# Moving the last three output products of a head pair's upper tiles behind the next step's scores

## The reference

```python
h = layernorm(x) * (1 + ca) + sa
q = rope(h @ Wq.T)                    # 32 heads of 128
c_kv = h @ Wdk.T                      # shared low rank part of keys and values
k = [rope part from h @ Wkr.T, rest from c_kv @ Wupk.T]   # 8 key heads
v = c_kv @ Wupv.T                     # 8 value heads, 4 query heads share one
a = softmax(causal(q @ k.T / sqrt(128))) @ v
x = x + ga * (a @ Wo.T)
h = layernorm(x) * (1 + cb) + sb
s = softmax(h @ router_w.T + router_b)        # 64 experts, the 8 largest kept as w
x = x + gb * (h * sum(w) + w @ expert_bias)
```

## Time and profile before

| | us |
|---|---|
| median of 3 runs (lowest, highest) | 1481.37 (1480.51, 1482.84) |
| profiled execution, time | 1481.78 |
| profiled execution, span from first to last instruction | 1480.1 |
| TensorE busy | 1451.2 (98% of the span) |
| its weight loads busy | 1211.3 (82%) |
| VectorE busy | 1160.1 (78%) |
| GpSimd busy | 1023.6 (69%) |
| ScalarE busy | 1005.0 (68%) |

### The profile page before, as it was taken

How to read it: one execution, slowest core, us unless ns; L and a number is a source line. 1 busy time by engine, 2 the same in 40 slices (tenths; PEclk the granted TensorE clock), 3 DMA queues, 4 the chain that set the end, 5 groups by cost and what they waited for, 6 DMA issues and landing times.

```text
span 1480.1 us, 24295 instructions
## 1 busy us (share of the span) xinstructions
PE 1451.2 (98%) x7012; PEld 1211.3 (82%) x7012; DVE 1160.1 (78%) x3549; ACT 1005.0 (68%) x2381; POOL 1023.6 (69%) x802
## 2 busy tenths in 40 slices
PE   7997999999999999999999999999999999999997
PEld 4686888888888888888888888888888888888876
DVE  5867777777777777777777777777779988988866
ACT  2467776776767776777677766767677676776674
POOL 1656776776667776677678666767588888886662
PEclk9999999999999999999999999999999999999999
DMA  9647775776766676578667756669788899889881
GB/s 328 205 126 255 223 229 144 213 224 182 202 216 214 181 223 188 172 219 237 182 184 222 220 168 199 213 180 254 224 248 252 270 293 260 278 263 266 268 228 51
DMA packets 214820, 322.02 MB, mean 218 GB/s; under 512 B 42248, under 2 KB 132104, under 8 KB 214688
## 3 DMA queue, kind: packets, MB, share of 16 engines
q1 hardware_dynamic: 214352, 320.34, 72.3%
q10 hardware_dynamic: 336, 0.12, 0.0%
HBM read 179.43 MB, written 140.95 MB: 216 GB/s over the span
## 4 chain that ended last, share of the span: by engine, by line
PE 90%; DVE 5%; issue 2%; ACT 2%; POOL 1%; DMA 0%; SPq 0%; DVEq 0%; ACTq 0%; POOLq 0%
PE bank_s L589 22%; PE bank_o L718 22%; PE bank_pv L696 14%; PE bank_s L649 13%; PE bank_s L617 6%; PE bank_s L602 5%; PE bank_s L560 2%; PE bank_o L523 1%; PE bank_s L645 1%; PE bank_s L771 1%; DVE blocks L1417 1%; ACT probs L1028 1%; PE bank_pv L589 1%; DMA wup_in<-in_wup 0%; PE bank_s L646 0%
## 5 line engine op out<-in xcount | busy, mean ns | idle before, releaser
L1759 POOL TENSOR_TENSOR PT_lo<-PT_raw,PT_hi 128x640 fp32r<-128x640 f32 x246 | 382.1, 1574 | 27.0 <-ACT PT_hi L1049 27.0
L1035 ACT ACTIVATE probs<-probs,row_inv 128x512 f32<-128x512 f32 (+3 forms) x512 | 258.0, 553 | 195.2 <-DVE row_inv L1400 195.1
L1747 POOL TENSOR_TENSOR rot_c<-rot_c,rot_s 128x512 f32<-128x512 f32 x128 | 166.0, 1297 | 274.3 <-DVE rot_s L1357 274.3
L1028 ACT ACTIVATE probs<-probs,row_min 128x512 f32<-128x512 f32 (+3 forms) x512 | 281.8, 552 | 52.2 <-DVE row_min L1393 52.1
L1417 DVE STREAM_TRANSPOSE blocks<-probs 128x384 f32<-128x384 f32 x508 | 213.9, 447 | 18.7 <-ACT probs L1035 12.4
L649 PE MATMUL bank_s<-kT_both,qT_hi 128*128 128x512 f32 (+2 forms) x768 | 214.9, 341 | 1.2 <-POOL qT_lo L1752 0.6
L1393 DVE CUSTOM_DVE_ANT_0 probs<-bank_s,mask 128x512 f32<-128x512 f32 (+2 forms) x384 | 203.5, 552 | 0.4
L589 PE MATMUL bank_s<-hT_lo,wq_hi 128*128 128x512 f32 x488 | 196.5, 403 | 2.5 <-DVE row_min L1393 1.2
L1752 POOL TENSOR_TENSOR qT_lo<-rot_c,qT_hi 128x512 fp32r<-128x512 f32 x128 | 166.6, 1301 | 42.2 <-ACT qT_hi L1010 41.3
L718 PE MATMUL bank_o<-wo_lo,OT_hi 128*128 128x512 f32 x496 | 194.4, 392 | 0.0
L718 PE MATMUL bank_o<-wo_hi,OT_hi 128*128 128x512 f32 x496 | 193.3, 390 | 0.0
(11 more groups left out here) (296 smaller groups left out, 3216.6 us busy)
## 6 DMA issues: line engine op xcount, KB each, us to landing
blocks<-blocks SPq DMA_DIRECT2D x127, 640.0 KB, 3.4
PT_raw<-blocks SPq DMA_DIRECT2D x500, 160.0 KB, 3.9
stage<-in_wq SPq DMA_DIRECT2D x32, 256.0 KB, 5.1
vblocks<-kv_raw SPq DMA_DIRECT2D x32, 256.0 KB, 5.4
kv_raw<-vblocks SPq DMA_DIRECT2D x128, 64.0 KB, 2.1
stage<-in_wo SPq DMA_DIRECT2D x32, 256.0 KB, 5.0
split_wq<-wq_hi SPq DMA_DIRECT2D x32, 256.0 KB, 5.4
split_wq<-wq_lo SPq DMA_DIRECT2D x32, 256.0 KB, 5.7
```

The source lines that it names most:

```text
L1028: ins = act.activation(row(t, qt), row(t, qt), ACT.Exp, bias=row_min[m][:, qt:qt + 1], scale=-1.0, accum_out=row_sum[m][:, qt:qt + 1])
L1035: ins = act.activation(row(t, qt), row(t, qt), ACT.Copy, scale=row_inv[t % 2][:, qt:qt + 1])
L1747: pool.tensor_tensor(rot_c[:], rot_c[:], rot_s[:], ALU.add).then_inc(pool_a, 1)
L1759: pool.tensor_tensor(lo[:, at], raw_of(t)[:, at], hi[:, at].bitcast(F32), ALU.subtract).then_inc(pool_t, 1)
```

## The change

In the 61 even steps t = 4 to 124, the last three of the twelve output products of the upper tiles (tile 3, second head of the pair) are no longer issued at the end of the odd step; the even step issues them between its scores and its query projection. The semaphores that tell that the upper tiles' products are done (`pe_op`, `pe_upper`) are counted up there. ScalarE's copy of the lower tiles moves from the start of the even step to between the exponentials of tiles 3, 2 and those of tiles 1, 0, and VectorE's half moves behind the maxima of tiles 1 and 0. No instruction is added or removed.

```diff
+            def upper_in_two(p):
+                return p < PAIRS - 2
+
             def out_pair(p, tiles, some=None):
...
                     for h in heads:
-                        o_at = (2 * (j - tiles[0]) + h % 2) * P
-                        for n, (o, w) in enumerate(passes(OT_of(p, tiles), wo)):
-                            mm = pe.matmul(bank[f"o{j}"][:], o[:, o_at:o_at + P], w[:, h, :], ...)
-                    if heads[1] == GROUP - 1:
-                        mm.then_inc(pe_op, 1)
-                    elif j == UPPER[-1]:
-                        mm.then_inc(pe_upper, 1)
+                        if j == UPPER[-1] and h == heads[1] and upper_in_two(p):
+                            return
+                        out_head(p, tiles, j, h)
+
+            def out_head(p, tiles, j, h):
+                u = 2 * p // GROUP
+                o_at = (2 * (j - tiles[0]) + h % 2) * P
+                for n, (o, w) in enumerate(passes(OT_of(p, tiles), wo)):
+                    mm = pe.matmul(bank[f"o{j}"][:], o[:, o_at:o_at + P], w[:, h, :], ...)
+                if h == GROUP - 1:
+                    mm.then_inc(pe_op, 1)
+                elif h == 1 and j == UPPER[-1]:
+                    mm.then_inc(pe_upper, 1)
...
# TensorE, step
                 scores(t + 1, QUERY_ORDER, before, n)
                 if h % 2 == 1 and t > 1:
                     values_pair(t // 2 - 1, LOWER)
+                if h % 2 == 0 and t > 2 and upper_in_two(t // 2 - 2):
+                    p = t // 2 - 2
+                    out_head(p, UPPER, UPPER[-1], 2 * p % GROUP + 1)
                 if 2 < t < ALL - 3:
                     q_proj(t + 3)
...
# ScalarE, step
-                if h % 2 == 0 and 2 < t < ALL - 2:
-                    pair_split_hi(t // 2 - 2, LOWER)
...
                 exponentials(t + 1, 0)
                 if h == 1 and t > 1:
                     v_split_hi(u)
+                if h % 2 == 0 and 2 < t < ALL - 2:
+                    pair_split_hi(t // 2 - 2, LOWER)
                 exponentials(t + 1, 1)
...
# VectorE, step
+                mask_and_max(t + 1, 1)
                 if h % 2 == 0 and 2 < t < ALL - 2:
                     pair_split_lo(t // 2 - 2, LOWER)
-                mask_and_max(t + 1, 1)
```

More of the change, by code:

```diff
@@ L715, in out_pair @@
                     for h in heads:
-                        o_at = (2 * (j - tiles[0]) + h % 2) * P
-                        for n, (o, w) in enumerate(passes(OT_of(p, tiles), wo)):
-                            mm = pe.matmul(bank[f"o{j}"][:], o[:, o_at:o_at + P], w[:, h, :],
-                                           start=(u < LAST_UNIT and h == 0 and n == 0),
-                                           stop=(u < LAST_UNIT - 1 and h == GROUP - 1 and n == 2))
-                    if heads[1] == GROUP - 1:
-                        mm.then_inc(pe_op, 1)
-                    elif j == UPPER[-1]:
-                        mm.then_inc(pe_upper, 1)
+                        if j == UPPER[-1] and h == heads[1] and upper_in_two(p):
[5 more added lines that the diff above has]
+                for n, (o, w) in enumerate(passes(OT_of(p, tiles), wo)):
+                    mm = pe.matmul(bank[f"o{j}"][:], o[:, o_at:o_at + P], w[:, h, :],
+                                   start=(u < LAST_UNIT and h == 0 and n == 0),
+                                   stop=(u < LAST_UNIT - 1 and h == GROUP - 1 and n == 2))
+                if h == GROUP - 1:
+                    mm.then_inc(pe_op, 1)
+                elif h == 1 and j == UPPER[-1]:
+                    mm.then_inc(pe_upper, 1)
             def values_last(t, tiles):
```

## The result

| | before | after |
|---|---|---|
| median of the runs, us | 1481.66 (4 runs, 1480.51 to 1482.84) | 1495.52 (4 runs, 1494.23 to 1496.88) |
| profiled execution, us | 1481.78 | 1495.23 |
| its span, us | 1480.1 | 1493.6 |

The ratio of the times is 1.0094, with a 95% interval of 1.0076 to 1.0111: the change makes the kernel 13.9 us slower. The forecast was 1496.5.

A forecast was written before the change was run, and what follows sets the result against it. It took TensorE's own work (busy 98%) as the bound. Terms -5.5 + 6.8 + 9.8 + 4.1 = +15.2 us on 1481.78 gave 1497.0, stated as 1496.5 for the median; range by its bounds 1490 to 1502, 8 in 10 1484.5 to 1502.

The forecast's parts named there:

- gap after the scores: TensorE, even steps: moved products fill its wait before the query projection, net 0.09 us in 61 steps, 5.5 us gain.
- key wait, quiet h = 2: Scores' tile 2: earlier weight load waits for VectorE's key rotation, 0.31 us lost in 22 steps, 6.8 us.
- late copies, t = 4 to 92: Lower output products wait for copies behind exponentials where a DMA holds ScalarE's split: 6.5 + 0.3 + 0.6 + 1.4 us.
- late copy at t = 124: Step t = 124: the split's DMA landing is late again, so the lower copy is too, 1.0 us lost.
- router steps, over the gap gain: Steps t = 94 to 122, VectorE nearly full: key and value waits lose 4.1 us, bounds 1 and 9.
- VectorE's own queue: 0: Inverses and query rotation queued behind VectorE's moved half of the copy: its idle time absorbs the hold, 0 us.
- 0.2 us in all: Late copies in the router steps: router products give them over a microsecond more, so only 0.2 us is lost.
- Rival D: Knock-on: VectorE's held queue delays rotations and landings, twenty more late steps at 0.5 us, 1506, or 1511 with slow clock; chance 0.08.
- B: Rival: key wait happens, but copies stay hidden as DMAs land earlier, +5 us, 1486; chance 0.15.
- C: Rival: lower copies come late but the scores have no key wait, +5 us, 1487; chance 0.05.
- A: Rival: only the gaps after the scores go, so faster by 5.5 to 9 us, 1474; chance 0.09.
- clock part of D: TensorE drops to the slow clock after ten waits of over half a microsecond, 1.5 us each, giving 1511.

The follow-up runs named there:

- E4: The changed kernel with ScalarE's copy of the lower tiles placed between the split and the exponentials of tiles 3 and 2; 1484.82 us.
- E6: The kernel of E4 with one product moved in the steps h = 2 instead of three, still three in h = 0; 1477.57 us.
- E1: The kernel before with only the two copies of the lower tiles moved as in the change, the three products left in the odd step; 1493.16 us.
- E9: The kernel before, no product moved: ScalarE's copy between split and exponentials, VectorE's half behind the maxima of tiles 1 and 0; 1481.64 us.
- E8: The kernel before with only VectorE's half of the lower tiles' copies moved, behind the maxima of tiles 1 and 0; 1480.76 us.
- E12: The changed kernel with one product moved in the steps h = 2 instead of three, copies left as in the change; 1491.06 us.
- E7: The kernel of E4 with two products moved in the steps h = 2 instead of three; 1479.96 us.

## Why the prediction was right, and where it was right only in its sum

By its own terms, each with what the runs showed for it:

| term | forecast | shown | from |
|---|---|---|---|
| gap after the scores | -0.09 x 61 = -5.5 | -6.5 | 45 quiet steps at about -0.115 (E4, E6), 16 router steps taken at -0.08, from E4's t = 104, 108, 116 and 124 |
| key wait, quiet h = 2 | +0.31 x 22 = +6.8 | +6.3 | (0.165 + 0.123) x 22, E4 less E6 |
| late copies, t = 4 to 92 | +8.8 | +8.3 | lengths of after less E4 |
| late copy at t = 124 | +1.0 | 0 | after is 0.09 shorter than before there |
| router steps, over the gap gain | +4.1 | +6.2 | 4.9 + 16 x 0.08 |

With the start's -0.6 the third column gives 13.7, the span's 13.5. The sum, 15.2, is near this partly by luck. Terms that were too high by 5.9 us together (gap 1.0, key wait 0.5, late copies in the quiet steps h = 0 0.9, at t = 4 1.1 and at t = 124 1.0, key and value waits of the router steps 1.4) stand against terms that were too low by 5.0 (late copies in the quiet steps h = 2 1.4 and in the router steps 3.6).

**The gap** was right in mechanism and 1 us too small: I set aside 0.04 of the gain for a slow pitch behind the scores, and did not need all of it. E6 adds what I had not seen: one product of the three is enough.

**The key wait** was right in place, number and size: rotation's end plus 0.05 for the load and 0.29 more for the second product, as worked out from the earlier trace rows; 22 loads. By the Trainium skill, page "TensorE: Matmul & The Clock Gate", section "Part 2: What happens when you issue a matmul", weight loads are pulled ahead of running products. That did not make the key wait vanish: the 22 loads of the kernel after wait for VectorE, 0.46 us each.

**The late copies** were right in mechanism (E1, E4, E9: ScalarE's place behind the exponentials, in steps whose split a DMA holds), and the sum of the quiet steps only looks right. It is made of two errors. At t = 4 I took 1.4; the landing came earlier, ScalarE's copy started at 136.01 (136.56 on the scale of the kernel before) instead of about 137.3, and 0.3 was lost. For the steps h = 2 I took 0.6 in two steps; it was 2.0, mostly in four (t = 30, 42, 66 and 82, with 0.29, 0.93, 0.25 and 0.43). The steps h = 0 came out at 5.9 (nine steps with over 0.2) against 6.8 forecast. The rule for one step held. By it a late step loses the split's start less 0.53, that is less 1.22 now that the scores start 0.69 earlier (and less 0.30 more in a step h = 2). In these thirteen steps (t = 8, 20, 28, 40, 52, 60, 72, 84 and 92, and the four of h = 2) the split starts 1.35 to 2.37 us after the first score product, and after less E4 is 0.05 to 0.09 more than the rule in each; for t = 60 it is 0.48, with 0.5 forecast. But which steps are late the profile of before did not tell: of the eight steps h = 0 that I counted, t = 16 and 64 lost under 0.1, t = 28, 84 and 92 were late instead, and E1 has another ten.

**The router steps.** Here two steps of the prediction failed: "VectorE's own queue: 0", and "0.2 us in all" for the late copies, which the sum of 4.1 does not even hold. In the quiet steps the first one stands: VectorE's half behind the maxima costs nothing while ScalarE's is in time (E8). In the router stretch VectorE is busy 230 of 258 us. A lower copy that is late holds what is queued behind it, and one step on the upper copy is late as well and TensorE waits for its bank (the rows at 1131.49 and 1140.51). I had looked only for TensorE's wait at the lower output products, which the router products do hide: one load waits there, for 0.2 us. The kernel of E4 has +1.4 in these steps and the kernel after +4.9, so 3.6 us there are late copies. (With the 8.3 of the quiet steps that makes 11.9 by one profile of each; the medians of the two kernels are 10.7 apart.) The rest, 1.4 + 1.3 = 2.7 over the gap gain, is less than my 4.1. Rival D had this mechanism, at quiet steps and 0.5 us each, and was mostly wrong in place.

**The other rivals.** None of them happened, but the experiments made them: E4 is B (copies hidden), 1484.8, where I gave 1486; E12 is C (no key wait), 1491.1 for 1487; E6 is nearest to A (only the gaps go), 1477.6 for 1474. Their prices were right to about 4 us. The clock part of D did not happen: from 145 to 1050 us TensorE stood idle seven times for a late copy, up to 0.8 us, and behind the longest of the new waits, 1.29 us at t = 119, the granted clock is 1.00 as well. The lower level, 1.2 GHz, is granted behind a longer wait that both kernels have at t = 126, where TensorE waits 2.6 us for VectorE's `PT_lo`, so it is no part of the difference. Before and after (length, busy per engine, clock, DMA share, GB/s):

```profile
1437.50:1440.00 2.50, 2.50 (x8) 2.11 (x9) 0.00 (x1) 2.25 (x5) 0.00 (x0) 0.51 0.66 184
1451.10:1453.00 1.90, 1.90 (x6) 1.61 (x7) 0.06 (x2) 1.86 (x4) 0.00 (x0) 0.50 0.96 238
```

The Trainium skill, page "TensorE: Matmul & The Clock Gate", section "HAM oscillation — how this bites in real kernels", warns that idle gaps bring the slow clock back; the trace agrees for the wait of 2.6 us and shows nothing of it for the waits that the change adds.

## What to carry to other kernels

Ask of an operation that is moved into a gap how small it may be: one product of 0.23 us closed a gap of 0.10 to 0.15, the second and third only ate the room of the next consumer. Before moving a copy behind other work on a queue, look for the steps in which that work itself waits for a transfer; on average ScalarE had a third of its time free, and twenty steps out of 61 still paid. Ask too what stands behind the copy on an engine that is itself nearly full: there the delay is paid one step later, at another bank. When a wait is removed by reordering an engine that has no slack at that place, expect it to come back under another name.

## What was not expected of the hardware

**A late weight load costs less than it waits.** Waits of 0.24 and 0.46 us cost 0.06 and 0.29 us of the step (E7 and E4 against E6): 0.17 to 0.18 us less than the wait in both. In E6, with nothing left of the room by the count of products, the load for tile 2 starts in time.
